# Row maxima of attention scores in chunks of 512 keys, with one job for the last 66 keys of four query tiles

## What is computed

```python
x = layer_norm(layernorm(x)) ; q = x @ Wq ; k, v = split(context @ Wkv)     # 16 heads of 64
k, v = concat([null_k, k]), concat([null_v, v])                             # 1602 keys
sim = einsum('bhid,bhjd->bhij', q * s, k * s)                               # 2048 x 1602 a head
attn = softmax(where(mask, sim, -max))
out = layer_norm((attn @ v) @ Wout)
```

## Time and profile before

| | |
|---|---|
| time, median of 3 runs | 1411.72 us (1411.37 to 1411.84) |
| span of the profiled execution, first to last instruction | 1409.9 us |
| TensorE: busy share of the span, matmuls | 98%, 7984 |
| GpSimd | 68% |
| VectorE | 49% |
| ScalarE | 45% |
| mean granted TensorE clock | 1.000 |

### The profile page before, as it was taken

The page is one execution under the profiler, slowest core; times in us unless marked ns, Lnnn a source line. Parts: engine busy times, 40 slices in busy tenths (PEclk is TensorE's granted clock), DMA queues, the critical chain, the costliest instruction groups (busy, mean ns, idle before and its releaser), DMA issues.

```text
span 1409.9 us, 20726 instructions
## 1 busy us (share of the span) xinstructions
PE 1378.2 (98%) x7984; PEld 772.6 (55%) x7984; DVE 697.4 (49%) x966; ACT 640.6 (45%) x776; POOL 957.2 (68%) x485
## 2 busy tenths in 40 slices
PE   7999999999999999999999999999999999999998
PEld 3345555455554555454555555554555556877876
DVE  5445554554555545554545554555545545454542
ACT  3334445454544444444445444444446444233232
POOL 1028889888988998899889888988899671110100
PEclk9999999999999999999999999999999999999999
DMA  5240001000100010001001100100140220112000
GB/s 153 76 145 1 17 17 47 16 17 16 47 16 17 17 54 16 13 27 41 16 16 23 48 16 16 47 17 17 46 132 16 76 76 16 52 39 75 1 16 15
DMA packets 54997, 53.82 MB, mean 38 GB/s; under 512 B 13745, under 2 KB 41332, under 8 KB 54900
## 3 DMA queue, kind: packets, MB, share of 16 engines
q1 hardware_dynamic: 49044, 47.39, 11.0%
q10 hardware_dynamic: 5856, 5.11, 1.2%
HBM read 34.79 MB, written 17.56 MB: 37 GB/s over the span
## 4 chain that ended last, share of the span: by engine, by line
PE 88%; ACT 9%; issue 1%; DMA 1%; DVE 1%; SPq 0%; DVEq 0%; ACTq 0%
PE ps_o L1416 28%; PE ps_s L1403 21%; ACT prob L863 7%; PE ps_x L1518 7%; PE ps_x L1282 7%; PE ps_s L1518 4%; PE ps_o L1335 4%; PE ps_s L1282 3%; PE ps_s L1490 3%; PE ps_o L1352 2%; PE ps_s L1268 2%; PE ps_o L1324 2%; PE ps_o L1326 2%; PE ps_s L1270 2%; PE ps_x L1294 1%
## 5 line engine op out<-in xcount | busy, mean ns | idle before, releaser
L664 POOL TENSOR_TENSOR acc<-acc,prob 128x1024 f32<-128x1024 f32 x342 | 814.3, 2381 | 96.8 <-ACT prob L863 55.8
L1028 DVE TENSOR_REDUCE mxh<-ps_x 128x2 f32<-128x804 f32 x408 | 406.7, 997 | 515.9 <-PE ps_x L1282 515.7
L863 ACT ACTIVATE prob<-ps_s,keybias 128x1024 f32<-128x1024 f32 x416 | 440.6, 1111 | 255.1 <-PE ps_s L1403 255.1
L1416 PE MATMUL ps_o<-prob,vp 128*64 128x512 f32 x1664 | 402.9, 605 | 1.5 <-DMA vp<-v_scratch 1.5
L1416 PEld LDWEIGHTS ps_o<-prob,vp 128*64 128x64 f32 x1664 | 100.9, 136 | 174.3 <-issue 165.3
L1403 PE MATMUL ps_s<-ql,kh 64*128 64x512 f32 x832 | 165.3, 392 | 0.0
L1403 PE MATMUL ps_s<-qh,kh 64*128 64x512 f32 x832 | 165.1, 392 | 0.0
L1403 PE MATMUL ps_s<-qh,kl 64*128 64x512 f32 x832 | 164.7, 391 | 0.0
L1282 PE MATMUL ps_x<-kh,qh 64*128 64x402 f32 x816 | 162.8, 394 | 1.8 <-DVE mxh L1028 1.2
L1403 PE MATMUL ps_s<-shift,one_sel 64*128 64x512 f32 x832 | 164.2, 389 | 0.0
L664 POOL TENSOR_TENSOR acc<-prob 128x1024 f32<-128x1024 f32 x32 | 75.9, 2372 | 129.1 <-issue 92.1
(11 more groups left out here) (160 smaller groups left out, 1229.7 us busy)
## 6 DMA issues: line engine op xcount, KB each, us to landing
rb<-r_scratch SPq DMA_DIRECT2D x64, 128.0 KB, 2.9
o_scratch<-o_sb SPq DMA_DIRECT2D x32, 256.0 KB, 2.0
otb<-o_scratch SPq DMA_DIRECT2D x4, 2048.0 KB, 7.9
v_scratch<-vsb SPq DMA_DIRECT2D x13, 512.0 KB, 3.2
vp<-v_scratch SPq DMA_DIRECT2D x8, 832.0 KB, 5.0
xs<-in_x SPq DMA_DIRECT2D x4, 512.0 KB, 6.9
xres<-in_x ACTq DMA_DIRECT2D x1, 2048.0 KB, 10.4
out<-obuf SPq DMA_DIRECT2D x8, 256.0 KB, 2.1
```

What stands on the lines that cost most here:

```text
L664: gp.tensor_tensor(a, so_far, term, ALU.add).then_inc(sums_p, 1)
L863: act.activation(prob[:, slot(u, s), :, :], ps_s[s % S_BUFS][:, :, :], ACT.Exp, bias=keybias[:, kt:kt + 1], scale=SCALE).then_inc(p_made, 1)
L1028: dve.reduce_max(mxh[:, :, qt, quarter], ps[:, :, 0:MXW], AX.X).then_inc(x_free, 1)
L1416: last = pe.matmul(ps_o[qb % 2][rows(g), :], vp[u][:, kt, rows(g)], prob[:, slot(u, s), g, :], start=(kt == 0), stop=(kt == KT - 1))
```

## The change

The chunk width MXW goes from 402 to 512 keys. Three chunks cover 1536 keys of a query tile (jobs 0 to 11 of a block, three a tile), and job 12 covers the last 66 keys of all four query tiles: eight matmuls of 66 columns, four for each head, side by side in the head's bank. VectorE reduces that job to eight numbers at once; the fourth column of mxh takes them. A block thus has 13 jobs, a pair 52, which is two in each cycle. The bank jobs and `SA_THREE` go, with their waits on p_made and x_free; in the loop every job is in ps_x. The last pair's stream is 33 jobs, and the head's 19, still alternating between the two buffers. The cycles of all spare jobs stay.

```diff
--- before.py
+++ after.py
@@ -35,7 +35,10 @@
 CAUG = CDIM + 2
 C1 = CAUG - P
 KCH = KPAD // 4
-MXW = 402
+MXW = 512
+MXF = KEYS // MXW
+MXR = KEYS - MXF * MXW
+MXJ = 4 * MXF + 1
 QH = QT // 2
 FF = 1024
 FK = FF // P
@@ -50,7 +53,7 @@
 BY_TENSOR = {QB * PAIRS - 1: (11, 12)}
 
 assert STEPS % 2 == 0 and (STEPS - RING // 2) % RING == 0
-assert 4 * MXW >= KEYS and 4 * MXW <= KPAD and KPAD % 4 == 0
+assert MXF == 3 and 0 < MXR and MXR % 2 == 0 and 4 * MXR <= 512 and KPAD % 4 == 0
 
 
 CT_N = (KT + 1) // 2
@@ -59,20 +62,19 @@
 
 
 K_AT, Q_AT, MX_AT, L_AT, C_AT = (3, 5, 6, 8), (11, 12, 16, 19), (23, 4, 10, 17), (9, 15, 22, 2), (17, 18)
-SA_THREE = {2, 3, 6, 7, 8, 9, 12, 13, 15, 20, 21, 22}
 RECIP_AT = (11, 17, 24, 4)
 HEAD_SA = 6
 
 
 def plan_pair(first, last):
 
-    plan = [{"pre": [], "post": [], "bank": [], "C": [], "spare": []} for _ in range(CYCLES)]
-    stream = [(0, qb, j) for qb in range(1, QB) for j in range(16)][HEAD_SA:]
+    plan = [{"pre": [], "post": [], "C": [], "spare": []} for _ in range(CYCLES)]
+    stream = [(0, qb, j) for qb in range(1, QB) for j in range(MXJ)][HEAD_SA:]
     if not last:
-        stream += [(1, 0, j) for j in range(16)] + [(1, 1, j) for j in range(HEAD_SA)]
+        stream += [(1, 0, j) for j in range(MXJ)] + [(1, 1, j) for j in range(HEAD_SA)]
     x = 0
     for c in range(CYCLES):
-        for where in ("pre", "post", "bank") if c in SA_THREE else ("pre", "post"):
+        for where in ("pre", "post"):
             if x < len(stream):
                 plan[c][where].append((x, stream[x]))
                 x += 1
@@ -114,7 +116,7 @@
 
     for c in range(4):
         order += queries(c)
-    for j in range(16):
+    for j in range(MXJ):
         order += [("SA", 0, j), next(values)]
     for j in range(HEAD_SA):
         order += [("SA", 1, j), next(values)]
@@ -1020,13 +1022,15 @@
             def maxima(j, job, pair, ps):
 
                 dn, qb, i = job
-                qt, quarter = i // 4, i % 4
                 at = x_count(j, pair)
                 if i == 0 and pair is not None or qb:
                     dve.wait_ge(mx_made, blocks(0 if pair is None else pair[0] + dn, qb))
                 dve.wait_ge(x_made, at + 1)
-                dve.reduce_max(mxh[:, :, qt, quarter], ps[:, :, 0:MXW], AX.X).then_inc(x_free, 1)
-                if i == 15:
+                if i < MXJ - 1:
+                    dve.reduce_max(mxh[:, :, i // MXF, i % MXF], ps[:, :, 0:MXW], AX.X).then_inc(x_free, 1)
+                else:
+                    dve.reduce_max(mxh[:, :, :, MXF], ps[:, :, 0:4 * MXR].rearrange("p g (t k) -> p g t k", k=MXR), AX.X).then_inc(x_free, 1)
+                if i == MXJ - 1:
                     dve.wait_ge(x_free, at + 1)
                     if pair is None:
                         dve.wait_ge(init, 11)
@@ -1126,8 +1130,6 @@
                             rest_of_queries(job[2], j, pair)
                     for j, job in plan[c]["post"]:
                         maxima(j, job, pair, ps_x)
-                    for j, job in plan[c]["bank"]:
-                        maxima(j, job, pair, ps_s[0])
                     if last and c == C_AT[0]:
                         add_four(n, u, 2)
                     for j, i in plan[c]["C"]:
@@ -1273,14 +1275,20 @@
 
                 dn, qb, i = job
                 n, _, u = pair if pair is not None and dn == 0 else after(pair)
-                qt, quarter = i // 4, i % 4
                 if i == 0:
                     pe.wait_ge(q_hi, QB * n + qb + 1)
                 if i == 0 and qb == 0:
                     pe.wait_ge(k_hi, 4 * (n + 1))
-                for g in range(2):
-                    last = pe.matmul(ps[:, g, 0:MXW], qh[u][rows(g), (4 * qb + qt) * P:(4 * qb + qt + 1) * P],
-                                     kh[u][rows(g), quarter * MXW:(quarter + 1) * MXW], start=True, stop=True)
+                if i < MXJ - 1:
+                    qt, chunk = 4 * qb + i // MXF, i % MXF
+                    for g in range(2):
+                        last = pe.matmul(ps[:, g, 0:MXW], qh[u][rows(g), qt * P:(qt + 1) * P],
+                                         kh[u][rows(g), chunk * MXW:(chunk + 1) * MXW], start=True, stop=True)
+                else:
+                    for t in range(4):
+                        for g in range(2):
+                            last = pe.matmul(ps[:, g, t * MXR:(t + 1) * MXR], qh[u][rows(g), (4 * qb + t) * P:(4 * qb + t + 1) * P],
+                                             kh[u][rows(g), MXF * MXW:KEYS], start=True, stop=True)
                 last.then_inc(x_made, 1)
 
             def attn_out_0(i, j):
@@ -1446,20 +1454,14 @@
                     pe.wait_ge(init, 11)
 
                 for c in range(CYCLES):
-                    taken = plan[c - 1]["bank"] if c else []
                     for j, job in plan[c]["pre"]:
-                        pe.wait_ge(x_free, x_count(j, pair) - len(taken))
+                        pe.wait_ge(x_free, x_count(j, pair))
                         maxima(j, job, pair, ps_x)
-                    for j, job in taken:
-                        pe.wait_ge(x_free, x_count(j, pair) + 1)
                     scores(n, u, 2 * c)
                     scores(n, u, 2 * c + 1)
                     for j, job in plan[c]["post"]:
                         pe.wait_ge(x_free, x_count(j, pair))
                         maxima(j, job, pair, ps_x)
-                    for j, job in plan[c]["bank"]:
-                        pe.wait_ge(p_made, S_BUFS + STEPS * n + 2 * c + 1)
-                        maxima(j, job, pair, ps_s[0])
                     for j, i in plan[c]["C"]:
                         attn_out_0(i, j)
                     if c:
```

## The result

The changed kernel takes 1385.61 us (1385.07 to 1386.14, four runs) beside 1411.78 for the kernel before in the same comparison: 0.9817 of it, 95% interval 0.9803 to 0.9831. The forecast was 1383.0, in a range from 1379 to 1398. The gain is 26 us where 28.7 were forecast.

What follows compares the result with a forecast made beforehand. TensorE's queue, busy 98% of 1409.9 us, was taken as the bound; -52.1 + 17.7 + 7.1 - 1.7 + 0.3 = -28.7 us gave 1383.0 us, range 1379 to 1398 with rivals A (up to the 0.23 pitch) and B.

Steps and rivals of the forecast that it cites:

- (a): Loop: removing 93 bank jobs (maxima jobs in the score bank) at 0.56 us each takes 52.1 us off TensorE.
- (b): Long maxima jobs: 512 columns for 402 cost 0.046 us more each, 17.7 us in sum.
- (c): Tail job: 32 of them, four matmul pairs each at a load-set pitch of 0.11 us, cost 7.1 us in sum.
- (d): Head: 19 jobs for 22 between value projections, three fewer, -1.7 us.
- (e): VectorE: longer reductions, at most 1.27 us, stay covered by about 0.3 and over 0.4 us, so cost nothing.
- (g): GpSimd: 126 us a pair against TensorE's 131.1; only the last pair waits, for otb, 0.3 us charged.
- A: Tail job: load and stream take turns, pitch 0.155 us, 5.8 us more, 1388.8; chance 0.13.
- D: Tail job: pairs don't overlap at all, pitch 0.45 us for 0.11, 43.5 us more, 1426.5; chance 0.03.
- C: ps_x comes free late: reductions of 1.7 us make TensorE wait, about 1411 to 1424 us; chance 0.03.
- B: GpSimd takes over: exp waits for a slot or TensorE for row sums; 1387 at 0.5 us a pair; chance 0.05.

Runs made afterwards that it cites:

- The two bank-place runs: Changed kernel with the second job of twelve cycles put back in the score bank: 1435.98 us; the same with 402-column jobs and a one-pair tail: 1410.30 us.
- the two runs on the tail's pitch: Changed kernel with tail matmuls for only one of four query tiles: 1375.88 us; with tail matmuls of 128 keys in place of 66: 1385.95 us.
- the run at 128.2 us a pair: Changed kernel with long jobs of 402 columns and the tail job as one pair of 402 columns: 1361.74 us, 0.9654 of the kernel before.

## Why the prediction was right, and where it was off

*Bound and mechanism.* Right. TensorE's queue is the path, a pair shrinks from 134.7 to 131.47 us (forecast 131.1), and the bank term carries the gain.

*(a), 0.56 us a bank job.* Right in the sum, a little high (6.50 for 6.72 a pair, some 1.5 us over seven pairs: 0.54 a cycle, where I read 0.56), and wrong in its reading. I called it 0.185 of streaming and the rest wait and restart. The two bank-place runs show that in such a cycle the exponential sets the end and a job behind the scores is free. It made no odds for the sum, which took the cycle's whole difference, but it made my first expectation for the bank places wrong by 20 us.

*(b), 0.046 us a long job.* Mis-sized: 0.050, some 1.2 us over seven pairs. It was counted as columns by clock; the timelines show 0.05 at the job ahead of the scores (0.29 to 0.34 us to the next matmuls) and 0.06 between the job behind them and the values (0.27 to 0.33). Why the second is more was not tried. The plain cycle of 4.39 to 4.40 us stands right at the 4.4 above which the prediction would have called the term upset.

*(c), the tail.* Right: pitch 0.11, 0.86 us a pair for 0.88. The nearest row, short matmuls with a load each, was the right guide. The Trainium skill's sentence in "TensorE: Matmul & The Clock Gate", section on packing small matmuls, that a load overlaps a matmul only where row groups differ, is again not what this trace shows: the tail's loads for the same half of the rows follow each other by 0.11 us whether 66 or 128 columns stream between them, which they could not if load and stream took turns.

*(d), the head.* 0.7 us net forecast, 0.9 seen.

*(e), VectorE.* Right, from both sides: shorter reductions gain nothing, 0.7 us more costs 91, and the cover is 0.36 and 0.46 us where 0.3 and over 0.4 were counted. Only the sign given for trouble, weight loads that wait for VectorE, was badly chosen, since the kernel before shows it too (60.8 us).

*(g), GpSimd and otb.* The wait is where it was put (0.3 us charged, 0.8 and 0.2 in two executions), but that is luck: the step was wrong. From the last pair's first scores GpSimd's side came to the load 0.3 us sooner and not 0.5 later (71.02 us after them for 71.28), and TensorE came to its use 2.5 us sooner and not 3.0 (79.80 for 82.32). At 7.9 us for the load 0.9 us of slack would have been left. The wait came from a longer load, which the prediction did not have. The last pair gained 1.7 us where 2.7 were forecast; about half a microsecond of that is this wait.

*The rivals.* A and D fell by the two runs on the tail's pitch, C by the shorter reductions, B by the run at 128.2 us a pair. Yet the table of waits seems to speak for B: it lists ScalarE's exponentials as waiting 12.9 us in 14 places for GpSimd, a line that the kernel before did not have. Here is one, with an earlier one, in ScalarE's timeline:

```profile
606.52 2.12 ACT L865 ACTIVATE prob<-ps_s,keybias 128x1024 f32<-128x1024 f32 x2 [0.75 <-PE ps_s L1411]
...
611.12 2.12 ACT L865 ACTIVATE prob<-ps_s,keybias 128x1024 f32<-128x1024 f32 x2 [1.09 <-POOL acc L666]
```

The exponential at 611.12 waited 1.09 us, and the one at 581.91, at the same kind of place behind another copy of ScalarE's, waited as long (1.08) with the scores named. The profile names the releaser that came last by its events. By the kernel's own order the addition that frees this slot is the first of its block, and in GpSimd's timeline that one ended at 595.97, 15 us before. So this row is no wait for GpSimd, and the pair's 131.47 us, all covered by TensorE, leave no room for one.

## What to carry to other kernels

A job that borrows a buffer from a pipeline costs what the pipeline's own release costs, not what the job streams: read its price from the difference of two whole cycles, one with and one without it. Before counting the jobs saved, ask which of them lay beside that wait, for they are saved for nothing. And when a single buffer is to carry all jobs, compare its turnaround with the distance between jobs, not the engine's busy share: a VectorE that was busy half the time had 0.36 to 0.46 us to give, no more.

## What the runs showed that I had not expected

Two jobs in a cycle can take as long as three (4.84 and 4.83 us), with the third beside an exponential of 1.12 us. The same 2 MB load took 7.7 to 8.1 us or 8.8 to 9.5, and the longer ones were all issued between 1083.7 and 1084.6 us. And a short matmul's cost reaches over to its neighbour: behind a tail job the scores' second pair came 0.32 us after the first, not 0.23. The prediction had this in its sum (0.25 us for a tail job ahead of the scores, 0.19 for one behind them), but not where it would show.
